# Attention stages of a Trainium2 kernel: the first norm of the second chunk of tokens goes from step 1 into the stage's head

## What is computed

```
x = x + 0.5 * _L0_ffn_ref(_layernorm(x), ...)

def _layer(x, wqkv, qs, ksc, wo, lg, lb, w1, b1, w2, b2):    # DEPTH = 2 of them
    h = shift_token(x)              # half of the features come from the token before
    q, k, v = split(h @ wqkv)       # 8 heads of 64
    q = l2norm(q) * qs; k = l2norm(k) * ksc
    q, k = rotary_xpos(q, k)
    o = local_attention(q, k, v)    # windows of 64, each sees itself and the one before
    x = x + o @ wo
    h = layernorm(shift_token(x)) * lg + lb
    a, g = split(h @ w1 + b1)
    return x + (a * gelu(g)) @ w2 + b2
```

## Time and profile before

| | |
|---|---|
| Median of 3 executions | 1125.36 us |
| Lowest and highest | 1124.89 and 1128.22 us |
| The profiled execution: its own time | 1124.78 us |
| Its span, from the first to the last instruction | 1123.0 us |
| Instructions | 26079 |
| PE busy | 978.7 us, 87% of the span |
| DVE busy | 733.0 us, 65% |
| ACT busy | 686.3 us, 61% |
| POOL busy | 524.6 us, 47% |
| Mean clock granted to TensorE | 0.942 of full speed |

### The profile page before, as it was taken

The page is one execution under the profiler, slowest core; times in us unless marked ns, Lnnn a source line. Parts: engine busy times, 40 slices in busy tenths (PEclk is TensorE's granted clock), DMA queues, the critical chain, the costliest instruction groups (busy, mean ns, idle before and its releaser), DMA issues.

```text
span 1123.0 us, 26079 instructions
## 1 busy us (share of the span) xinstructions
PE 978.7 (87%) x9072; PEld 628.4 (56%) x9072; DVE 733.0 (65%) x1689; ACT 686.3 (61%) x1329; POOL 524.6 (47%) x392
## 2 busy tenths in 40 slices
PE   4889999999998968789999999999828996856995
PEld 1445555555555347255555555556428994435995
DVE  1678787787877554378777877778674442665442
ACT  3577686686684572577776776684615663834661
POOL 2555466566442515455444544552463550263552
PEclk9899999999999987899999999999968998877998
DMA  5656464364444600355444444443331222012224
GB/s 180 165 152 144 114 162 115 86 143 114 93 98 104 78 1 3 91 118 115 111 99 97 114 105 98 103 110 82 133 112 53 69 75 82 19 49 66 68 68 127
DMA packets 89712, 109.99 MB, mean 98 GB/s; under 512 B 20368, under 2 KB 74384, under 8 KB 88816
## 3 DMA queue, kind: packets, MB, share of 16 engines
q1 hardware_dynamic: 82160, 91.17, 34.2%
q0 software_dynamic: 4544, 9.35, 2.4%
q10 hardware_dynamic: 2880, 7.81, 2.2%
HBM read 62.66 MB, written 12.07 MB: 67 GB/s over the span
## 4 chain that ended last, share of the span: by engine, by line
PE 74%; ACT 8%; DVE 7%; issue 4%; DMA 4%; POOL 1%; SPq 1%; ACTq 0%; DVEq 0%; POOLq 0%
PE banks L602 9%; PE banks L984 7%; PE banks L994 7%; PE banks L690 5%; PE banks L676 5%; PE banks L651 4%; PE banks L634 4%; PE banks L683 4%; PE banks L790 3%; PE banks L746 3%; PE banks L735 3%; PE banks L659 2%; PE banks L610 2%; DMA arena<-arena 2%; PE banks L1019 2%
## 5 line engine op out<-in xcount | busy, mean ns | idle before, releaser
L2142 POOL TENSOR_TENSOR arena<-arena 128x1024 f32<-128x1024 f32 x64 | 150.9, 2357 | 308.6 <-DVE arena L1735 302.4
L2131 POOL TENSOR_TENSOR arena<-arena 128x1024 f32<-128x1024 f32 x64 | 150.8, 2357 | 27.1 <-ACT arena L1244 27.1
L602 PE MATMUL banks<-arena 128*128 128x512 f32 x256 | 138.8, 630 | 7.1 <-DVE arena L1627 5.9
L1236 ACT ACTIVATE arena<-banks,arena 128x512 f32<-128x512 f32 x128 | 80.7, 682 | 102.0 <-PE banks L683 101.5
L2121 POOL DMA_INDIRECT moe_outs<-arena x78 | 80.9, 1037 | 96.2 <-DVE arena L1986 88.6
L1470 ACT ACTIVATE arena<-banks,arena 128x128 f32<-128x128 f32 x312 | 89.0, 369 | 56.3 <-PE banks L984 56.3
L1727 DVE TENSOR_REDUCE arena<-banks 128x4 f32<-128x512 f32 x128 | 82.4, 685 | 56.7 <-PE banks L634 56.6
L2114 POOL DMA_INDIRECT moe_rows<-arena x64 | 63.7, 996 | 87.0 <-DVE arena L1708 66.7
L1735 DVE TENSOR_TENSOR arena<-arena 128x1024 f32<-128x1024 f32 x64 | 77.9, 1218 | 23.4 <-DMA arena<-arena 23.4
L994 PE MATMUL banks<-arena 128*128 x624 | 86.4, 281 | 3.3 <-ACT arena L1470 2.8
L984 PE MATMUL banks<-arena 128*128 128x128 f32 x624 | 86.8, 284 | 0.3 <-issue 0.2
(11 more groups left out here) (230 smaller groups left out, 1944.3 us busy)
## 6 DMA issues: line engine op xcount, KB each, us to landing
arena<-arena SPq DMA_DIRECT2D x256, 128.0 KB, 3.7
arena<-rstd SPq DMA_DIRECT2D x128, 256.0 KB, 4.3
arena<-moe_rows SPq DMA_DIRECT2D x78, 64.5 KB
arena<-in_mw SPq DMA_DIRECT2D x2, 2048.0 KB
arena<-moe_outs SPq DMA_DIRECT2D x16, 256.0 KB, 4.9
arena<-in_rot ACTq DMA_DIRECT2D x12, 256.0 KB, 3.3
arena<-in_wa ACTq DMA_DIRECT2D x2, 1026.0 KB, 6.7
arena<-ssm_a SPq DMA_DIRECT2D x4, 512.0 KB, 6.2
```

Source lines behind the costliest of these rows:

```text
L602: mm(bank[k], w_qkv[d][:, w0:w0 + P], (YA, YM)[d][:, c * C:(c + 1) * C], start=True, stop=True).then_inc(proj, 1)
L2131: nc.gpsimd.tensor_tensor(TA[:, n % 2], RAW, ROTV[:, :, 0, c * C:(c + 1) * C], ALU.mult).then_inc(cos_done, 1)
L2142: nc.gpsimd.tensor_tensor(TA[:, n % 2], TA[:, n % 2], TB, ALU.add).then_inc(rot_sum, 1)
```

## The change

The norm of chunk 1 leaves step 1 on PE, ACT and DVE and goes into the head, woven with that of chunk 0. On PE both centring products come first, then the two variance products; on ACT both squares, then both roots; on DVE the multiplication of chunk 1 comes behind that of chunk 0 and, in the first stage, behind the copies of the mask. Both variances use bank 5, so the second waits on one more semaphore, `ln_log`, until ACT has read the first. No operation is added or dropped, and SP and POOL are as they were.

```diff
--- before.py
+++ after.py
@@ -339,7 +339,7 @@
             return slice(L * (1 - q % 2), L * (2 - q % 2)), DD * (q % 2) + 16 * (q // 2)
 
         LN_CEN, LN_VAR = (4, 6, 7, 7), (5, 5, 2, 2)
-        LN_STEP = {1: 1, 4: 2, 5: 3}
+        LN_STEP = {4: 2, 5: 3}
         MLP_LAST = ((0, 5), (6, 7), (0, 5))
         MLP_BANKS = ((2, 7), (1, 7), (2, 2))
         MX_TOK, MX_RANK = [(0, 3, 3, 7), (7, 6, 3, 7)], [(1, 4, 4, 6), (3, 4, 5, 4)]
@@ -550,6 +550,8 @@
 
             def first_variance(n0, c):
                 need(pe, ln_sq, n0 + c + 1)
+                if c == 1:
+                    need(pe, ln_log, n0 + 1)
                 mm(bank[LN_VAR[c]][:], mean, MSQ if c else sq[:, 0], start=True, stop=True).then_inc(ln_var, 1)
 
             def centred(src, c, to=None):
@@ -800,8 +802,6 @@
                         pe.wait_ge(sq_done, n)
                         pe.wait_ge(x_ffn, NCH + 1)
                         token_rows(0, 0)
-                    if s == 1:
-                        first_centred(norm0, 1, run)
                     if s >= 4:
                         transpose_out(s - 4, n - 4, s)
                     if s >= 3:
@@ -810,8 +810,6 @@
                             values(s - 3, n - 3, 1)
                     if s < STEPS:
                         square_sum(s, n)
-                    if s == 1:
-                        first_variance(norm0, 1)
                     if s >= 2:
                         masks(s - 2, n - 2)
                         scores(s - 2, n - 2)
@@ -1111,7 +1109,9 @@
                     if run:
                         centred_router()
                     first_centred(norm0, 0, run)
+                    first_centred(norm0, 1, run)
                     first_variance(norm0, 0)
+                    first_variance(norm0, 1)
                     ffn(norm0, run)
                 elif kind == "S":
                     ssm()
@@ -1309,9 +1309,6 @@
                         if hp == 0 and g >= 2:
                             evacuate_out(s - 4, n - 4)
                         inverse_norm(n)
-                    if s == 1:
-                        first_square(norm0, 1)
-                        first_root(norm0, 1)
                     if s >= 4 and not (hp == 0 and g >= 2 and s < STEPS):
                         evacuate_out(s - 4, n - 4)
                     if s in (4, 5):
@@ -1543,7 +1540,9 @@
             for k, (kind, norm0, run) in enumerate(plan):
                 if kind == "F":
                     first_square(norm0, 0)
+                    first_square(norm0, 1)
                     first_root(norm0, 0)
+                    first_root(norm0, 1)
                     ffn(norm0, run)
                 elif kind == "S":
                     ssm()
@@ -2090,6 +2089,7 @@
                     nc.vector.tensor_copy(MASK, OT[:, 0:3].rearrange("p h n -> p (h n)"))
                     nc.vector.tensor_copy(IDENTB, ident).then_inc(mask_done, 1)
                 if kind == "F":
+                    norm_chunks(norm0, shifted, [1])
                     for y in (YB, YM):
                         last = nc.vector.memset(y[DH:P, 0:1], 0.0)
                     ffn(norm0, run)
```

## The result

| | before | after |
|---|---|---|
| Median (20 executions each, taken in turns) | 1126.43 us | 1130.05 us |
| Lowest and highest | 1124.00 and 1130.59 | 1124.44 and 1132.57 |
| The profiled execution: its own time | 1124.78 | 1129.81 |
| Its span | 1123.0 | 1128.0 |
| PE, DVE, ACT, POOL busy, us | 978.7, 733.0, 686.3, 524.6 | 979.1, 732.8, 687.2, 524.9 |

The ratio of after to before is 1.0026, with a 95% interval from 1.0014 to 1.0038: some 2.9 us slower by the mean times, between 1.6 and 4.3 (the medians lie 3.6 us apart). That is real and too small to count as a difference by the bound of 0.3%. The forecast was +0.8 us. The sums of busy time moved by less than 1 us on every engine and the mean clock by 0.001, so most of it is in waits and in where the clock is low.

The account below looks back on a forecast made before the run. PE bounds the kernel (74% of the last-ending chain); at the two stage starts all engines wait for one another. 4.8 - 1.8 - 1.0 + 0 - 1.2 = +0.8 us on 1125.36 gave 1126.2 us, range 1122.0 to 1130.5.

Parts of the forecast that it names:

- Head of stage 1, delay: First stage's start: PE, in order, waits for the second load of x, delaying everything behind by 4.8 us.
- Head of stage 1, clock: First stage's start: projection of step 0 runs at full clock, -1.8 us; bounds 0 and -1.8.
- Stage 1, cp1-cp2: First stage, step 1's ACT copies to step 2's: gain cut by transfers, -1.0 us; bounds 0 and -3.1.
- Stage 1, cp2-sq3 (a rival): First stage, step 2's copies to step 3's square: 0 us; if the clock falls, +1.8 to +4.3 per stage, chance 0.18.
- Head of stage 2: Second stage's start: taken as 0 us; -1.4 us, if the clock stays full, kept for the range.
- Stage 2, cp1-cp2: Second stage, step 1's ACT copies to step 2's: gain limited by the swap's landing, -1.2 us; bounds 0 and -3.1.
- the net that the prediction put 3.0 us lower: First stage's start: by the skill's DMA rule the delay would be 1.8 us, the net 3.0 us lower; not adopted.
- the rival on the clock: Step 2, both stages: clock falls as PE does less; +1.8 to +4.3 us per stage, 1129.8 to 1134.8 us, chance 0.18.
- the prediction's own sign of being wrong: At `project_v`: the forecast is wrong if PEclk drops below 0.8 over its eight passes.
- The argument against the rival: Step 2: the earlier projection and the scores still fill more than half of the stretch, against a clock fall of chance 0.18.

Follow-up runs that it names:

- kernel with x early: The change, with the second chunk of x loaded right behind the first, ahead of the rotary tables; 0.9976 of the time of the kernel before.
- the repeat: The unaltered change profiled a second time, in a timed run; 1.0011 of the time of the kernel before, first stage 332.8 us.
- the third: The unaltered change profiled a third time, in a single execution; 1132.71 us, first stage 336.3 us.
- the first stage alone: The kernel before, with the move made in the first attention stage only; 1.0057 of its time, first stage 335.1 us.
- PE was filled: The change, with products of no use put into PE's waits in steps 1 and 2 of both stages; 1.0046 of the time of the kernel before.
- the repaired move: The change, with x's second chunk loaded early and the first stage's second rotary pair issued in step 2; 0.9971 and 0.9944 of the kernel before.
- an unmoved first stage with x early: The kernel before, with the move in the second stage only and x's second chunk loaded right behind the first; 0.9966 of its time.

## Why the prediction was right and wrong

The result lies in the range, on the side that was forecast, and is no difference by the bound of 0.3%, as forecast; the size was off: +0.8 predicted, +2.9 measured. The steps, as the prediction put them:

| Step | predicted | in after's profile | mean of 4 |
|---|---|---|---|
| Head of stage 1, delay | +4.8 | +4.9 | +4.9 |
| Head of stage 1, clock | -1.8 | -1.6 | -1.2 |
| Stage 1, cp1-cp2 | -1.0 | +0.2 | +0.9 |
| Stage 1, cp2-sq3 (a rival) | 0 | +2.8 | +1.3 |
| Head of stage 2 | 0 | -1.6 | -1.9 |
| Stage 2, cp1-cp2 | -1.2 | -0.8 | +0.3 |

(The third column is against the single profile before, the fourth against the mean of the three that did not move the norm. Pieces behind `sq3` differ by up to 2 us between executions of one kernel and are left out.)

**Head of the first stage: right.** PE in order behind the landing of x, four passes at 1.2 GHz, the projection at 19.0: it came at 19.06. The kernel with x early shows the cause. The load of x landed 5.7 us after its issue in after, and 6.0 when issued first, so the net that the prediction put 3.0 us lower would have been further off. The section of the Trainium skill that the prediction took it from (DMA: Bandwidth & Descriptors, "Anatomy of one DMA") gives its fit for transfers that GpSimd issues. SyncE issued this load, among others, so it is no test of that fit as the section states it.

**The clock in that head: right in two executions of four.** The projection took 1.98 us in after and in the repeat, 3.51 and 3.66 us in the third and in the first stage alone. I took the best bound as the value; the mean of the four is 2.78 us, so -1.0. (The table's columns go on to the copies of step 1, and differ from these figures by 0.2 us.)

**Step 1 of the first stage: mis-sized, and then wrong in sign.** That the freed loads would collide with the swap was right, and `copy_out(2)` did wait for DMA. The landing went from 3.8 to 6.2 us (5.9 in the repeat) and not to 5.1: the bytes of the pair over the rate of an otherwise empty stretch, 1.35 us, were too little for what they cost a transfer that shares the engines with them, 2.1 to 2.4 us against the 3.8 before. With it the term is +0.2 and not -1.0. The second half of the error is in the base: the earlier trace rows give 9.2 us from copies to copies, and the other two profiles without the move 8.3, so a part of the wait I meant to win was not there in them.

**Steps 2 and 3 of the first stage: the rival on the clock came true there.** Priced at +1.8 to +4.3 per stage, it cost +2.8 in after and some 1.5 in two others, and nothing in the repeat. By the prediction's own sign of being wrong, PEclk under 0.8 over the eight passes of `project_v`, this step failed: it read 0.50 up to 46 us and 0.68 from 46 to 48. The argument against the rival, that the earlier projection and the scores still fill more than half of the stretch, held and did not help: from 30.09 to 41.17 PE was idle for 1.4 + 1.2 + 1.4 us, about a third, and the clock stayed low. What the prediction passed over is that the variance it took away had stood right in front of the projection. In the five profiles that keep the norm of chunk 1 in step 1 of the first stage `project_v` took 1.98 to 2.09 us, in the nine without it 1.98 to 3.78 us, 1.98 in two of them. That the missing passes do it is argued from these rows, not shown by a run. In the second stage, where I priced it alike, `project_v` took 1.98 us in three of four. The Trainium skill (TensorE: Matmul & The Clock Gate, "A second HAM failure mode: psum-queue depth-cycling") says of one kernel that frequent short idles between its groups of products make the clock oscillate. That agrees with two levels within one step here; it doesn't tell after from its repeat, 3.78 and 1.98 us for the same four passes of the same program.

**Head of the second stage: the term taken as 0 was -1.6 to -1.9.** I chose between 0 and -1.4 by the nearest row, the stretch from 456 to 458 at which the clock had dropped again. In all eleven profiles with the move in this stage the projection of step 0 ran at 2.4 GHz, and in all three without it at 1.2. The step that failed is the choice of row: the earlier trace rows had the clock fall behind a wait of 2.96 us, and the move cuts exactly that wait into 0.87 and 0.99. The projection of step 1 got its full clock too, which I had not counted.

**Step 1 of the second stage: not worth its 1.2.** Against the single profile before it is 0.8 us shorter, against the mean not at all. The copies wait for the swap (landing 4.0 us after the issue, as forecast), but the two other profiles without the move took 6.8 and 7.1 us from copies to copies, where the projection of step 2 ran at 2.4 GHz (1.88 us, 2.88 in the profile I read). There the copies already came as the swap landed, and nothing was left to win. With the variance gone from in front of it, the projection took 3.6 us in after.

By after's own profile the table's column adds up to +3.9: the swap (+1.2 against the forecast) and the clock in steps 2 and 3 (+2.8) stand against the second head (-1.6), and the rest is 0.7 us. The mechanisms were named; which of two clock levels holds where was read from one execution, in both directions. That the total still fell into the range is in part luck: a cost taken as 0 (+2.8) and a gain taken as 0 (-1.6) partly cancel.

## What to carry to other kernels

Moving work out of a wait also moves what was issued behind it: look for the transfers that then go out early and what they share engines with; here 512 KB of loads that nobody awaited cost a swap on the path 2 us, and one line put it right. When a product is moved ahead in an engine that works in order, first move the load it needs. And take a term that hangs on TensorE's clock from several profiles: one profile gave 9.2 us for a step that took 8.3 in the next two.

## What was not expected of the hardware

- The same program's first stage took 332.8, 335.9 and 336.3 us in three executions, by what clock `project_v` and the projections met (PEclk 0.50 up to 40 us in one, up to 46 in another).
- The two passes of a variance, placed in an idle gap of 2.96 us, went with a full clock for the projection behind it in 11 of 11 profiles (1.2 GHz, for all or most of it, in the 3 without them); eight plus two passes of no use in the first stage did not keep it up to `project_v`.
- A load of 256 KB issued 5.4 us earlier took 6.0 us to land instead of 5.7 and did not delay the constants: the first centring started at 6.34 us either way. The mask landed 0.6 us later (14.7 against 14.1 us), and DVE waited 1.25 us for it, off the path.

What stays open: what decides between 1.98 and 3.78 us in step 2 of the first stage (compared over executions and kernels, not controlled by any), why the swap landed later still where PE was filled (copies 7.3 us after its last issue), and whether the repaired move beats an unmoved first stage with x early in total time.
